# One-hot windows of 32 nodes, one group each, in a four-layer graph network kernel

## The chip, the cores and the metric

The kernel runs on one core of one Trainium2 chip. The metric is the device time of one execution in microseconds (us), the median over several runs.

## The reference

Four layers on 625 nodes with 512 features and 20000 edges, whose target nodes `dst` are sorted. Each layer is applied to `relu(layernorm(x))` and added to `x`.

```
dst = (625 * jax.random.uniform(jax.random.fold_in(_gk, 3), (20000,)) ** 2.0).astype(jnp.int32)
_o = jnp.argsort(dst, stable=True); src = src[_o]; dst = dst[_o]
...
# layer 0: mean over incoming edges
agg = segment_sum(x[src], dst) / max(deg, 1);  out = relu(agg @ W_l.T + b_l + x @ W_r.T)
# layer 1: four transformer blocks with attention over the edges (4 heads, conditioned layer norm)
# layer 2: graph convolution, norm = dis[row] * dis[col] * sigmoid(edge_attr_3 @ conf_w.T + conf_b)
# layer 3: a network on every edge
h        = mish(concat([x[src], x[dst], edge_attr_64]) @ W1 + b1)
messages = mish(h @ W2 + b2)
agg      = segment_sum(messages, dst)
u        = mish(concat([x, agg]) @ W3 + b3);  out = layernorm(x + u @ W4 + b4) * gamma + beta
```

## The kernel before

The edges are cut, in their sorted order, into 40 **groups** of 512 (`GROUPS`), a group into four tiles of 128 edges. Since `dst` is sorted, a group has its targets in a short run of nodes. The kernel relies on that twice: a **window** of `WIN` nodes from the group's first target is compared with the targets of its edges, which gives a one-hot matrix only `WIN` columns wide, and a product with this matrix sums the edges onto the window.

- `front` builds the three dense 640 x 640 adjacency matrices (`sums`: counts, and weights in a high and a low part). VectorE (DVE) makes the source one-hots (`compare_from`, L607, three tiles of a group; ScalarE makes the fourth with `Abs` and `Relu`, L371 and L374) and the target one-hots (`compare_to`, L599). GpSimd (POOL) multiplies these by the edge weights (L350). TensorE (PE) multiplies source by target one-hots (L491, 20 matmuls a group) into PSUM, and DVE adds the result onto the window of `sums` (`add_span`, L627). Two groups (`SHARE = 2`) share a window of 64 nodes and one addition. The window's start is loaded from memory into a register of DVE's sequencer (`start_of`, L593, a TENSOR_LOAD with three small instructions).
- `transformer_and_gcn` is dense and isn't touched.
- `edge_layer` runs layer 3. POOL gathers the rows of both ends of each edge (L1756, L1787) by indirect DMA; PE turns them (L1861), adds the edge features (L1869, L1870) and multiplies by W2 (L223); ScalarE (ACT) and DVE compute two `mish` functions per pair of tiles (`step`, one step for each of 80 pairs, two steps a group); PE sums a group's messages onto its window (L1901, in two column halves of the array, `side`); DVE copies the sums out of PSUM (L2131), and POOL adds them onto the table in memory (L1801). The last four groups are summed in another way (L1885).

The width of the window is made safe by **sweeps**. The kernel takes the largest difference between a span's last and first target, counts in how many of the thresholds `WIN`, `2 WIN`, ... are at or below it, and loads that count `n` on each engine. All loops then run over `n + 1` times the 40 groups: sweep `w` repeats the whole work with each window moved on by `w * WIN` nodes.

```
step(dve.tensor_scalar(over[:, :], iota16[0:1, WIN:NP:WIN], span1[:, 0:1], None, ALU.is_le))
step(dve.tensor_reduce(span1[:, 1:2], over[:, :], AX.X, ALU.add))
with dve.Fori(0, n * (GROUPS // RING) + (GROUPS // RING - 1)) as t:           # front
with eng.Fori(0, n * (PAIRS // 4) + (PAIRS - DEPTH) // 4 - 1) as t:           # edge_layer, PAIRS = 80
```

Of the kernel before, what the change touches and what calls it, by code (L numbers as in the profile page):

```python
# [21 lines left out]
P = 128  # L22
# [13 lines left out]
SHARE = 2  # L36
# [3 lines left out]
WIN = 64  # L40
# [191 lines left out]
def front(nc, k):  # L232

    RING = 4
    PEELED = 5
    ctx = ExitStack()
    with ctx:
# [6 lines left out]
        shared = sb("shared", [1, 2, SPANS])  # L244
        wtab = sb("wtab", [1, (MAXSWEEPS + 1) * GROUPS])
# [8 lines left out]
        to_onehot = [sb(f"to_onehot{a}", [P, TPG, 3, WIN], F16) for a in range(RING)]  # L254
# [4 lines left out]
        own_part = sb("own_part", [P, NT, D])  # L259
        eps, neg_mean, var = k.eps, sb("neg_mean", [P, NT]), sb("var", [P, NT])  # L260
# [51 lines left out]
        with nc.Block() as block:  # L312
# [23 lines left out]
            def _(pool):  # L336
# [6 lines left out]
                with pool.Fori(0, n * (GROUPS // RING) + GROUPS // RING) as t:  # L343
                    for a in range(RING):
# [4 lines left out]
                        weights = wb[:, bass.ds((t * RING + a) % GROUPS * TPG, TPG), :]  # L349
# [119 lines left out]
            def _(pe):  # L469
# [10 lines left out]
                with pe.Fori(0, n * (GROUPS // RING) + GROUPS // RING) as t:  # L480
                    for a in range(RING):
# [4 lines left out]
                        first, last = a % SHARE == 0, a % SHARE == SHARE - 1  # L486
                        if first:
                            pe.wait_ge(added, t * (RING // SHARE) + (a // SHARE + 1))
                        for i in range(NT):
                            for j in range(TPG):  # L490
                                mm = pe.matmul(ps[a // SHARE % 2][:, i * 4 * WIN:i * 4 * WIN + 3 * WIN],  # L491
                                               from_onehot[a][:, j, i * P:(i + 1) * P],
                                               to_onehot[a][:, j, :, :].rearrange("p a b -> p (a b)"),
                                               start=(first and j == 0 and i % 2 == 0), stop=(last and j == TPG - 1 and (i % 2 == 1 or i == NT - 1)))
# [42 lines left out]
            def _(dve):  # L537
# [30 lines left out]
                own(dve.tensor_reduce(shared[:, 0, :], cols(ps_row[:, 0, :], SHARE), AX.X, ALU.min))  # L568
                step(dve.tensor_reduce(shared[:, 1, :], cols(ps_row[:, 1, :], SHARE), AX.X, ALU.max))
# [1765 lines left out]
```

## Time and profile before

| | us |
|---|---|
| median of 3 runs | 1642.54 (1638.32 to 1642.61) |
| the profiled execution | 1639.68 |
| its span, first to last instruction | 1638.0 |

| stretch of the span, us | what runs |
|---|---|
| 0 to 104 | windows, weights and the loop of `front` |
| 104 to 862 | the rest of `front`, transformer and graph convolution |
| 862 to 975 | tables and the first steps of `edge_layer` |
| 975 to 1545 | the steady part of the edge steps |
| 1545 to 1638 | last steps and the end |

The views name an engine's own work by its name (PE, DVE, ACT, POOL) and its sequencer's by a q behind it (DVEq). The time of an instruction runs from its start to its end, and successive ones on an engine may overlap by some tens of nanoseconds.

### The profile page before, as it was taken

How to read it: one execution, taken by the hardware profiler on the slowest of the kernel's cores; microseconds unless marked ns; L12 is line 12 of the kernel's file. 1: busy time of each engine (PE TensorE's matmuls, PEld its weight loads, DVE VectorE, ACT ScalarE, POOL GpSimd, SP SyncE). 2: the span in 40 equal slices, each digit the busy share in tenths (PEclk: the TensorE clock that was granted, in tenths of full speed). 3: DMA queues.
4: the chain of work that ended last, by engine and by line, in shares of the span. 5: the costliest groups of instructions: out<-in, count | busy, mean ns of one | idle time of the engine just before them, and what ended most of it. 6: DMA issues, size and time to landing. Idle time of an engine off the chain costs nothing. (4 is left out here: it accounts for less than half of the span.)

```text
span 1638.0 us, 25185 instructions
## 1 busy us (share of the span) xinstructions
PE 1549.4 (95%) x8530; PEld 1226.5 (75%) x8530; DVE 1193.1 (73%) x1976; ACT 1097.3 (67%) x1534; POOL 672.7 (41%) x498
## 2 busy tenths in 40 slices
PE   5789899999999999999999999999999999999987
PEld 4765586878788878877854778787878787888774
DVE  8977646555565646465623499999999999999967
ACT  9841546544554546444530599999999999999963
POOL 3410200120012001200302788888888888888601
PEclk9999899999999999999999999999999999999989
DMA  3001320022012201212106767777777777777710
GB/s 106 0 20 66 92 83 26 15 68 87 26 33 84 77 1 33 81 36 78 41 1 222 160 142 148 146 150 150 148 152 148 152 150 148 149 149 150 170 39 32
DMA packets 107048, 153.95 MB, mean 94 GB/s; under 512 B 42043, under 2 KB 47035, under 8 KB 106467
## 3 DMA queue, kind: packets, MB, share of 16 engines
q0 software_dynamic: 72832, 87.84, 28.4%
q1 hardware_dynamic: 34146, 65.21, 12.6%
q8 instruction: 41, 0.67, 0.2%
q14 instruction: 29, 0.23, 0.0%
HBM read 141.02 MB, written 11.73 MB: 93 GB/s over the span
## 5 line engine op out<-in xcount | busy, mean ns | idle before, releaser
L1787 POOL DMA_INDIRECT edge_gathered<-dst_table,edge_index x158 | 262.0, 1658 | 58.7 <-issue 54.4
L223 PE MATMUL edge_z2p<-edge_w_hi,edge_h_hi 128*128 128x512 f32 x628 | 253.3, 403 | 2.6 <-DVE edge_late L2117 2.6
L223 PE MATMUL edge_z2p<-edge_w_lo,edge_h_hi 128*128 128x512 f32 x628 | 249.0, 396 | 0.0
L223 PE MATMUL edge_z2p<-edge_w_hi,edge_h_lo 128*128 128x512 f32 x628 | 248.8, 396 | 0.0
L1756 POOL DMA_INDIRECT edge_gathered<-src_table,edge_index x158 | 201.8, 1277 | 85.4 <-POOL edge_index L1750 30.6
L977 POOL TENSOR_TENSOR h<-h,tr_row_b 128x512 f32<-128x512 f32 x40 | 59.3, 1520 | 271.4 <-ACT C L1222 271.1
L966 POOL TENSOR_TENSOR tr_cw<-w_c,tr_cw 32x1024 fp32r<-32x1024 f32 x7 | 16.6, 2375 | 348.7 <-ACT tr_cw L1182 348.7
L223 PEld LDWEIGHTS edge_z2p<-edge_w_hi,edge_h_hi 128*128 128x128 f32 x628 | 118.4, 189 | 42.0 <-issue 16.9
L223 PEld LDWEIGHTS edge_z2p<-edge_w_hi,edge_h_lo 128*128 128x128 f32 x628 | 118.5, 189 | 28.5
L223 PEld LDWEIGHTS edge_z2p<-edge_w_lo,edge_h_hi 128*128 128x128 f32 x628 | 118.5, 189 | 25.0
L2134 DVE SCALAR_TENSOR_TENSOR edge_early<-edge_early,edge_z1p 128x1024 f32<-128x1024 f32 x79 | 96.4, 1220 | 48.9 <-ACT edge_early L2002 48.8
L993 PE MATMUL tr_one<-tr_yT_hi,tr_w_hi 128*128 128x256 f32 (+2 forms) x384 | 119.5, 311 | 4.4 <-issue 4.3
L993 PE MATMUL tr_one<-tr_yT_lo,tr_w_hi 128*128 128x256 f32 (+2 forms) x384 | 118.7, 309 | 0.0
L993 PE MATMUL tr_one<-tr_yT_hi,tr_w_lo 128*128 128x256 f32 (+2 forms) x384 | 118.7, 309 | 0.0
L1277 ACT ACTIVATE hT<-hT,tr_nmax 128x626 f32<-128x626 f32 x56 | 45.7, 817 | 95.3 <-DVE tr_nmax L1461 94.6
L2117 DVE TENSOR_TENSOR edge_late<-edge_z2p,w_c 128x512 f32<-128x512 f32 x157 | 101.7, 682 | 9.3 <-PE edge_z2p L223 5.0
L1998 ACT ACTIVATE edge_early<-edge_early 128x1024 f32<-128x1024 f32 x79 | 83.8, 1061 | 27.1 <-DVE edge_early L2090 26.9
L2145 DVE TENSOR_TENSOR edge_h_lo<-edge_early,edge_h_hi 128x1024 fp32r<-128x1024 f32 x79 | 96.8, 1225 | 2.7
L1075 PE MATMUL tr_two<-tr_kT,tr_qT 128*128 128x313 f32 x320 | 98.3, 433 | 0.2
L2097 DVE SCALAR_TENSOR_TENSOR edge_late<-edge_late 128x1024 f32<-128x1024 f32 x79 | 95.7, 1212 | 0.3 <-ACT edge_late L2011 0.3
L1461 DVE CUSTOM_DVE_ANT_0 hT<-tr_two,logc 128x626 f32<-128x626 f32 x80 | 64.6, 807 | 36.2 <-PE tr_two L1075 36.0
L2014 ACT ACTIVATE edge_late<-edge_late 128x1024 f32<-128x1024 f32 x79 | 84.0, 1063 | 4.6 <-DVE edge_late L2137 1.9
(366 smaller groups left out, 4020.0 us busy)
## 6 DMA issues: line engine op xcount, KB each, us to landing
w_c<-in_attr_T SPq DMA_DIRECT2D x78, 128.0 KB, 4.1
agg<-edge_sum_rows POOLq DMA_DIRECT2D x36, 128.0 KB, 10.7
w_a<-in_wv SPq DMA_DIRECT2D x4, 1024.0 KB, 5.3
w_b<-in_wq SPq DMA_DIRECT2D x4, 1024.0 KB, 5.4
w_a<-in_wk SPq DMA_DIRECT2D x4, 1024.0 KB, 7.7
w_b<-in_wo SPq DMA_DIRECT2D x4, 1024.0 KB, 6.8
w_a<-in_m SPq DMA_DIRECT2D x4, 1024.0 KB, 5.4
w_b<-in_m SPq DMA_DIRECT2D x4, 1024.0 KB, 5.5
```

What stands on the lines that cost most here:

```text
L223: mm = pe.matmul(out, a, b, start=(n == 0), stop=(n == last))
L993: mm = pe.matmul(out, a, b, start=(start and n == 0), stop=(stop and n == len(terms) - 1))
L1075: mm = pe.matmul(bank[:, f, 0:PART_A], qT[:, h, i * P:(i + 1) * P], kT[:, h, f * PART_A:(f + 1) * PART_A], start=True, stop=True)
L1461: ins = dve.tensor_tensor_reduce(out=cols(scores[n % 2][:, 0:USED], PART_A), in0=bank[:, :, 0:PART_A], in1=cols(k.logc[:, i, 0:USED], PART ...
L1756: pool.indirect_dma_start(out=from_rows[a][:, j, :].bitcast(F32), out_offset=None, in_=k.src_table, in_offset=bass.IndirectOffsetOnAxis(ap ...
L1787: pool.indirect_dma_start(out=from_rows[ring][:, j, :].bitcast(F32), out_offset=None, in_=k.dst_table, in_offset=bass.IndirectOffsetOnAxis ...
L1998: act.activation(m1[one], m1[one], ACT.Square).then_inc(S["inner1_ready"], 1)
L2014: act.activation(m2[two], m2[two], ACT.Square).then_inc(S["square2_ready"], 1)
L2097: dve.scalar_tensor_tensor(h2[new], m2[new], 0.5, z2[new], ALU.subtract, ALU.mult).then_inc(S["h2_ready"], 1)
L2117: dve.tensor_tensor(z2[two][:, j * D:(j + 1) * D], ps_z2[:, j * D:(j + 1) * D], b2, ALU.add).then_inc(S["z2_ready"], 1)
L2134: dve.scalar_tensor_tensor(m1[one], m1[one], 0.5, ps_z1[one][:, :], ALU.subtract, ALU.mult).then_inc(S["h1_ready"], 1)
L2145: dve.tensor_tensor(h1_lo[one][:, :, :], cols(m1[one], EDGE), h1_hi[one][:, :, :].bitcast(F32), ALU.subtract).then_inc(S["lo_ready"], 1)
```

## The change

`SHARE` goes from 2 to 1 and `WIN` from 64 to 32: each group has a window of its own, 32 nodes wide. With that:

- The largest difference is now taken over single groups and compared with 32, 64, ... (19 thresholds in place of 9); the table of starts has 840 entries in place of 440, is made by one instruction in place of ten, and is made again at the head of `edge_layer`.
- `front`'s loops run in turns of eight groups (`TO_RING = 8` buffers of target one-hots); `compare_to` is made six groups ahead (`TO_AHEAD`), the addition is one for each group, half as wide, and POOL's product for a group also waits until `compare_from` of the group two before it is done.
- `edge_layer` sums a group on PE in four column quarters of 32 in place of two halves of 64, with 128 output columns each in place of 256; the copy (L2131) and the addition in memory (L1801) have half the size.

```diff
-SHARE = 2
+SHARE = 1
-WIN = 64
+WIN = 32
+SIDES = P // WIN
+PLANES = D // (4 * WIN)
...
+    TO_RING = 8
+    TO_AHEAD = 6
...
-                        pool.wait_ge(to_ready, t * RING + (a + 1))
+                        pool.wait_ge(to_ready, t * TO_RING + (a + 1))
+                        pool.wait_ge(from_ready, t * TO_RING + (a + 1))
...
-                        pe.wait_ge(from_ready, u + 1)
+                        pe.wait_ge(from_ready, u + 3)
...
-                        if first:
-                            pe.wait_ge(added, t * (RING // SHARE) + (a // SHARE + 1))
+                        pe.wait_ge(added, u + 1)
...
+                own(dve.tensor_reduce(k.first_dst[:, :], cols(ps_row[:, 0, :], SHARE), AX.X, ALU.min))
+                step(dve.tensor_reduce(shared[:, :], cols(ps_row[:, 1, :], SHARE), AX.X, ALU.max))
+                step(dve.tensor_tensor(shared[:, :], shared[:, :], k.first_dst[:, :], ALU.subtract))
...
                 step(dve.tensor_scalar(over[:, :], iota16[0:1, WIN:NP:WIN], span1[:, 0:1], None, ALU.is_le))
...
-                with dve.Fori(0, n * (GROUPS // RING) + (GROUPS // RING - 1)) as t:
-                    for a in range(0, RING, SHARE):
-                        u = t * RING + a
-                        start, start_next = start_of(u), start_of(u + RING)
-
-                        dve.wait_ge(group_ready, u + (SHARE + RING))
-                        for b in range(SHARE):
-                            compare_to(u + (RING + b), a + b, start_next)
-                        add_span(t * (RING // SHARE) + a // SHARE, a, start)
-                        for b in range(SHARE):
-                            compare_from(u + (RING + b), a + b)
+                def group_step(u, a):
+                    start, start_ahead = start_of(u), start_of(u + TO_AHEAD)
+                    dve.wait_ge(group_ready, u + (1 + RING))
+                    compare_to(u + TO_AHEAD, (a + TO_AHEAD) % TO_RING, start_ahead)
+                    add_span(u, a, start)
+                    compare_from(u + RING, a % RING)
+
+                with dve.Fori(0, n * (GROUPS // TO_RING) + (GROUPS // TO_RING - 1)) as t:
+                    for a in range(TO_RING):
+                        group_step(t * TO_RING + a, a)
...
-                        pool.dma_start(k.agg[bass.ds(start, WIN), :].rearrange("n (s c) -> s n c", s=2),
+                        pool.dma_start(k.agg[bass.ds(start, WIN), :].rearrange("n (s c) -> s n c", s=SIDES),
...
-                                for side in range(2):
-                                    mm = pe.matmul(ps_sum[slot][side * WIN:(side + 1) * WIN, 0:D // 2],
+                                for side in range(SIDES):
+                                    mm = pe.matmul(ps_sum[slot][side * WIN:(side + 1) * WIN, 0:D // SIDES],
```

In DVE's program, inside `front`'s loop, half a turn (two groups) read before as follows; ISA stands for the sequencer's small instructions, `w_c` and `front_from_onehot` are the source one-hots of the two groups.

```order
L593 TENSOR_LOAD starts
L593 ISA x3
L593 TENSOR_LOAD starts
L593 ISA x2
L635 REGISTER_ALU
L599 ISA [waits front_group_ready]
L599 TENSOR_TENSOR front_to_onehot0<-front_iota16,front_dst16 128x4x64
L599 ISA
L599 TENSOR_TENSOR front_to_onehot1<-front_iota16,front_dst16 128x4x64
L625 ISA
L627 ISA [waits front_added]
L627 TENSOR_TENSOR front_sums<-front_sums,front_sum_ps0 128x15x64
```

In the same place one group reads now as follows, and every further group has the same rows again.

```order
L598 TENSOR_LOAD front_starts
L598 ISA x3
L598 TENSOR_LOAD front_starts
L598 ISA x2
L638 REGISTER_ALU
L604 ISA [waits front_group_ready]
L604 TENSOR_TENSOR front_to_onehot6<-front_iota16,front_dst16 128x4x32
L631 REGISTER_ALU
L633 ISA [waits front_added]
L633 TENSOR_TENSOR front_sums<-front_sums,front_sum_ps0 128x15x32
L612 ISA
L612 TENSOR_SCALAR w_c<-front_iota16,front_src_f 128x640
```

So the two loads of starts, which served two groups, now stand before each group; the comparison and the addition are half as large, and the addition comes once a group.

In PE's program, in a step of `edge_layer` that ends a group, the sums stood like this before, between the edge features and the product with W2:

```order
L1869 MATMUL edge_z1p<-edge_attr_parts,edge_attr_w_both 128x256
L1870 MATMUL edge_z1p<-edge_attr_parts,edge_attr_w_rest 128x256
L1901 MATMUL edge_sump<-edge_late,edge_onehot 64x256 x8
L223 MATMUL edge_z2p<-edge_w_hi,edge_h_hi 128x512
L223 MATMUL edge_z2p<-edge_w_lo,edge_h_hi 128x512
```

and stand like this now:

```order
L1879 MATMUL edge_z1p<-edge_attr_parts,edge_attr_w_both 128x256
L1880 MATMUL edge_z1p<-edge_attr_parts,edge_attr_w_rest 128x256
L1911 MATMUL edge_sump<-edge_late,edge_onehot 32x128 x16
L225 MATMUL edge_z2p<-edge_w_hi,edge_h_hi 128x512
L225 MATMUL edge_z2p<-edge_w_lo,edge_h_hi 128x512
```

Their place is the same; there are twice as many, each with a quarter of the output.

## Rows read from the trace of the kernel before

**Rows 1.** Busy time of each engine in five stretches of the span.

```profile
core 0: us, PE busy (x) PEld busy (x) DVE busy (x) ACT busy (x) POOL busy (x), PEclk, DMA share, GB/s
20.00:104.00 84.00, 67.37 (x780) 63.14 (x777) 81.51 (x169) 65.02 (x101) 36.68 (x36) 1.00 0.00 0
104.00:862.00 758.00, 722.12 (x3623) 570.86 (x3623) 440.02 (x877) 362.98 (x742) 84.15 (x53) 0.99 0.16 51
975.00:1545.00 570.00, 568.01 (x3279) 456.95 (x3274) 523.99 (x684) 543.78 (x548) 467.32 (x339) 1.00 0.77 152
```

**Rows 2.** Additions in front's loop, all of them (duration; first and last start).

```profile
L627 DVE TENSOR_TENSOR front_sums<-front_sums,front_sum_ps x20: 1137/1141/1155, 22.5 to 102.9; 128x960 f32 x20
```

**Rows 3.** Front's loop, instructions in time order: start, duration.

```profile
60.86 0.75 DVE L599 TENSOR_TENSOR front_to_onehot<-front_iota,front_dst 128x256 f16 x2
61.53 1.14 DVE L627 TENSOR_TENSOR front_sums<-front_sums,front_sum_ps 128x960 f32 x1
61.58 2.04 POOL L350 TENSOR_TENSOR front_to_onehot<-front_to_onehot,front_wb 128x512 f16<-128x512 f16 x2 [2.30 <-DVE front_to_onehot L599]
62.60 2.68 DVE L607 TENSOR_SCALAR front_from_onehot<-front_iota,front_src_f 128x640 f16<-128x640 f16 x6
...
65.20 0.74 DVE L599 TENSOR_TENSOR front_to_onehot<-front_iota,front_dst 128x256 f16 x2
```

**Rows 4.** Source and target one-hots of the whole loop: duration min/median/max.

```profile
L607 DVE TENSOR_SCALAR front_from_onehot<-front_iota,front_src_f x90: 371/374/1200, 13.7 to 99.6; 128x640 f16<-128x640 f16 x90
```

**Rows 5.** DVE's sequencer on L593, from 65.1 to 66.7: durations, first and last start.

```profile
L593 DVEq FUSED_REGOPS  x4: 53/124/190, 65.1 to 66.3; - x4
L593 DVEq TENSOR_LOAD <-starts x2: 311/311/311, 65.2 to 65.9; - x2
L593 DVEq SEQ_ASSERT  x2: 23/23/23, 65.8 to 66.5; - x2
```

**Rows 6.** DVE's sequencer, later in that half turn: L599, then L607.

```profile
L599 DVEq FUSED_REGOPS  x2: 131/133/135, 68.0 to 68.2; - x2
...
L607 DVEq FUSED_REGOPS  x6: 53/57/64, 68.7 to 69.3; - x6
```

**Rows 7.** Front's loop on PE and ACT, in time order.

```profile
61.85 1.81 PE L491 MATMUL front_sum_ps<-front_to_onehot,front_from_onehot 128*128 128x192 f16 x20
...
62.30 0.83 ACT L371 ACTIVATE front_away<-front_iota,front_src_neg 128x640 f16<-128x640 f16 x1 [0.75 <-PE front_sum_ps L491]
...
63.92 0.83 ACT L371 ACTIVATE front_away<-front_iota,front_src_neg 128x640 f16<-128x640 f16 x1
```

**Rows 8.** The chain that ended last, 1190 to 1220 us, by line.

```profile
by line: PE edge_z2p L223 73.6%; PE edge_sump L1901 10.0%; PE edge_z1p L1861 6.4%; PE edge_z1p L1869 5.5%; PE edge_z1p L1870 4.7%
```

**Rows 9.** Edge steps, 1041 to 1493 us: the second mish instruction of DVE, one a step.

```profile
L2134 DVE SCALAR_TENSOR_TENSOR edge_early<-edge_early,edge_z1p x55: 1220/1221/1224, 1040.6 to 1491.6; 128x1024 f32<-128x1024 f32 x55
```

**Rows 10.** Who waited for whom, 1041 to 1493 us: total, times, longest.

```profile
DVE edge_early L2134 <- ACT edge_early L2002: 29.7, 54, 0.8
...
ACT edge_early L1998 <- DVE edge_early L2090: 15.4, 27, 0.6
```

**Rows 11.** Two edge steps on DVE and ACT, in time order.

```profile
1191.02 1.22 DVE L2134 SCALAR_TENSOR_TENSOR edge_early<-edge_early,edge_z1p 128x1024 f32<-128x1024 f32 x1 [0.77 <-ACT edge_early L2002]
...
1199.09 1.22 DVE L2134 SCALAR_TENSOR_TENSOR edge_early<-edge_early,edge_z1p 128x1024 f32<-128x1024 f32 x1 [0.32 <-ACT edge_early L2002]
...
1203.53 0.87 DVE L2090 TENSOR_SCALAR edge_early<-edge_early 128x1024 f32<-128x1024 f32 x1
...
1204.43 1.06 ACT L1998 ACTIVATE edge_early<-edge_early 128x1024 f32<-128x1024 f32 x1 [0.57 <-DVE edge_early L2090]
...
1206.62 1.06 ACT L2002 ACTIVATE edge_early<-edge_early 128x1024 f32<-128x1024 f32 x1
```

**Rows 12.** A group's sums on PE, and the matmuls around them.

```profile
1205.49 0.28 PE L1870 MATMUL edge_z1p<-edge_attr_parts,edge_attr_w_rest 128*128 128x256 f32 x1
1205.75 1.95 PE L1901 MATMUL edge_sump<-edge_late,edge_onehot 128*64 128x256 f32 x16
1207.63 0.50 PE L223 MATMUL edge_z2p<-edge_w_hi,edge_h_hi 128*128 128x512 f32 x1
```

More of the change, by code:

```diff
@@ L611, in _ @@
                 dve.wait_ge(inputs_ready, 3)
-                for a in range(SHARE):
+                dve.sem_inc(from_ready, 2)
+                for a in range(2):
                     compare_from(a, a)
                 n = sweeps(dve)
-                for a in range(0, RING, SHARE):
-                    start = start_of(a)
-                    for b in range(SHARE):
-                        compare_to(a + b, a + b, start)
-                for a in range(SHARE, RING):
+                for a in range(2):
+                    compare_to(a, a, start_of(a))
@@ L620, in _, with add_span @@
+                for a in range(2, RING):
                     compare_from(a, a)
+                for a in range(2, TO_AHEAD):
+                    compare_to(a, a, start_of(a))
                 dve.wait_ge(sums_zero, NT)
-                def add_span(s, a, start):
-                    dve.wait_ge(added, s + 2)
+                def add_span(u, a, start):
+                    dve.wait_ge(added, u + 2)
                     into = sums[:, :, :, bass.ds(start, WIN)]
-                    dve.tensor_tensor(into, into, ps[a // SHARE % 2][:, 0:NT * 4 * WIN].rearrange(
+                    dve.tensor_tensor(into, into, ps[a % 2][:, 0:NT * 4 * WIN].rearrange(
@@ new lines, in _ @@
+                with dve.Fori(0, n * (GROUPS // TO_RING) + (GROUPS // TO_RING - 1)) as t:
+                    for a in range(TO_RING):
+                        group_step(t * TO_RING + a, a)
+                for a in range(TO_RING - RING):
+                    group_step(n * GROUPS + (GROUPS - TO_RING + a), a)
+                for a in range(TO_RING - RING, TO_RING):
+                    u = n * GROUPS + (GROUPS - TO_RING + a)
+                    start = start_of(u)
+                    dve.wait_ge(group_ready, u + (1 + RING))
+                    add_span(u, a, start)
@@ L1586, in edge_layer @@
         onehot = [sb(f"onehot{a}", [P, TPG, WIN]) for a in range(2)]
-        sum_rows = [sb(f"sum_rows{a}", [P, D // 2]) for a in range(2)]
+        sum_rows = [sb(f"sum_rows{a}", [P, D // SIDES]) for a in range(2)]
         own_part = sb("own_part", [P, KF, NP])
@@ L1766, in _ @@
                     gather_src(a)
+                pool.wait_ge(S["last_ready"], 1)
                 pool.wait_ge(dst_stored, 16 * NT)
@@ L2068, in _ @@
                 own(dve.tensor_copy(iota[:, :], iota_i[:, :]))
+                own(dve.memset(wtab[:, :], 0.0))
+                own.wait()
+                spans = [1, MAXSWEEPS, GROUPS]
+                own(dve.tensor_tensor(wtab[:, 0:MAXSWEEPS * GROUPS].rearrange("p (w g) -> p w g", g=GROUPS),
+                                      iota[0:1, 0:NP:WIN][:, :, None].to_broadcast(spans),
+                                      k.first_dst[:, None, :].to_broadcast(spans), ALU.add))
+                own.wait()
+                dve.tensor_scalar(starts[:, :], wtab[:, :], float(NP), None, ALU.min).then_inc(S["last_ready"], 1)
                 dve.wait_ge(S["made"], 2)
```

67 lines of the change are left out of this document (30 added, 37 removed).

## The prediction

> **What bounds the kernel now.** I read the busy times by stage first. In `front`'s loop DVE is busy 81.51 of 84 us, in the steady edge steps PE 568, ACT 544 and DVE 524 of 570 us; the 758 us between them are not touched by the change [rows 1]. So two places count.
>
> In `front`'s loop DVE's instructions follow each other without a gap: one turn of two groups runs from the comparison at 60.86 to the next at 65.20, 4.34 us or 2.17 a group [rows 3]. PE waits between groups and ACT has slack, two of its `Abs` lying 1.62 us apart [rows 7]. In the edge steps the chain that ended last runs over PE alone [rows 8]. But a busy PE is not the whole story: 54 of 55 times DVE's L2134 waited for ACT's L2002, 29.7 us in all, and ACT's L1998 waited for DVE's L2090 every second time, 15.4 us in all [rows 10]. Followed in time, L2134 at 1191.02 and at 1199.09 both wait for ACT, the next one comes after L1998, L2000 and L2002 end at 1207.68, and L1998 itself had waited for L2090 [rows 11]. That is a ring of DVE and ACT in which PE has no part, and it takes 8.1 and 8.6 us, together the period that the steps have: 451.0 us over 54 steps, 8.35 a step, 16.70 a group [rows 9]. PE and the ring are about equally long.
>
> **The change, part by part.** *The number of sweeps.* This decides everything else, so it comes first. A group needs a second sweep when its last target minus its first is 32 or more, since a window of 32 nodes holds a difference of 31. I drew `dst` as the reference does and cut it into groups of 512. The density of targets thins out towards the end (the square of a uniform number), and the differences grow from 0 in the first group to 28 to 32 in the last full ones. The largest is in the 39th group: nodes 590 to 622, a difference of 32. The threshold test is "32 at or below 32", which is true, so `n` becomes 1. Before, with pairs of groups, the largest difference is 59, below 64, and `n` is 0; the trace agrees, with 20 additions for 40 groups [rows 2] and one L2134 for each of 79 pairs. With `n` = 1 every loop that runs over groups, in `front` and in `edge_layer`, runs 80 groups in place of 40, whatever the window of a group holds: nothing is skipped. One node too many in one group of 40 costs a full second pass.
>
> *`front`'s loop, per group.* On DVE's own queue: the comparison of two groups takes 60.86 to 61.53, 0.67 us, so a half-sized one some 0.20; the addition lies 1.07 us ahead of what follows, half of it some 0.56; three clean source one-hots are 3 x 0.30 = 0.89, taking the starts within the six [rows 3]. Of the 90 and 30 such instructions the median is 374 ns, and one reached 1200 [rows 4]: it stood behind the addition while POOL's second product ran, 61.58 to 63.62 [rows 3]. The change puts POOL's product beside the addition, so I take all three clean. Sum 1.65 us a group. The Trainium skill (SBUF — State Buffer, "Who interferes with whom") says that DVE and GpSimd share a port pair as an exclusive lock and the loser blocks fully; by that rule this part should be a gain, of 0.4 us a group, and I have counted it so.
>
> But DVE's sequencer works too. It made the two loads of starts between 65.1 and 66.6, 1.5 us (TENSOR_LOADs at 65.2 and 65.9, the last assertion at 66.5) [rows 5]. The comparison's instruction takes 0.2 (68.0 to 68.2), from there to the source one-hots 0.5 for the second comparison and the addition, and these 0.13 each (68.7 to 69.3 for six) [rows 6]. Before, one pair of loads served two groups: 1.5 + 0.7 + 0.8 = 3.0 of 4.34 us, hidden under DVE's queue. Now every group has its own pair: 1.5 + 0.2 + 0.2 + 0.4 = 2.3 us, less a little where the groups' small instructions drop out, 2.25. That is longer than DVE's 1.65 and than ACT's 1.62, so I expect the sequencer to become the bound of this loop, at 2.25 a group; PE's 20 matmuls took 1.81 [rows 7] and can only get shorter with 96 columns in place of 192. The halved work saves nothing here. The first addition can start some 2 us earlier, at 20.5, as it needs one group and not two. 76 groups at 2.25 and the last four at PE's pace, 1.3 each, give 20.5 + 171 + 5 = 196.5. Before, the last addition ended at 104.0 [rows 2]. So **+93 us**. Bounds: 1.65 a group if the sequencer is somehow covered, +47; 2.4 if its extra waits cost time, +104.
>
> *Edge steps, per group.* The group's 16 matmul records take 1205.75 to 1207.63, 1.88 us [rows 12]. They come in two halves of the array side by side. With four quarters and half the columns the streaming halves: some 0.9 us less if four run side by side as two do, nothing less if they don't. DVE's copy of the sums halves too, by some 0.13. Since the ring of ACT and DVE stays as it is, PE's gain goes mostly into a wait of PE; I take 16.6 us a group in place of 16.70. The most that could come is a period of ACT's own busy time: 543.78 us in 570 [rows 1], which is 15.9 a group. The least is 16.8 (POOL's or PE's added instructions disturbing). The Trainium skill (TensorEngine Tiling (Array Packing), "Theoretical Speedup") promises up to 4x for at most 32 output columns of the stationary side; were PE the sole bound, that would give 0.9 us times 76 groups, 68 us, and more than ACT allows. The ring says otherwise, and that is a rival below.
>
> With a second sweep, 40 more groups run at the steady pace: 40 x 16.6 = 664 us; the 36 old ones in this form save 36 x 0.1 = 4. So **+660 us**.
>
> *The rest.* The table of starts (one instruction in place of ten, but 840 entries converted) comes out even to within 1 us; its second making at the head of `edge_layer` runs on DVE while PE's table products are long. The late groups' matmuls become smaller in columns, but not in weights. All of it I put at 0, with 2 us either way.
>
> **Sum.** 1639.7 (the profiled execution) + 93 + 660 = 2393 us. The profiled execution lies 3 us under the median, inside the spread of the three runs; I leave that out.
>
> **Rivals.**
>
> 1. *No second sweep* (the other side: not slower). All of the above hangs on one difference of 32. If the inputs on the chip have at most 31 in every group, `n` stays 0. For it: an older setting of the random generator draws other targets from the same seed, and with it I count a largest difference of exactly 31; nothing in this trace tells the two draws apart, as pairs of groups stay below 64 in both. A window chosen at 32 would fit such inputs. Against it: the generator as it stands gives 32. Then `front`'s loop ends at 20.5 + 36 x 2.25 + 5 = 106.5, +2.5 us, and the edge steps save 4: 1638, no change; if the ring gives way to ACT's 15.9 a group, 36 x 0.8 = 29 less, 1613. It decides between 31 and 32, with nothing between. 0.10, half of it on each of the two times.
>
> 2. *PE was the true bound in the edge steps*, as the chain of waits says [rows 8], and ACT's and DVE's waits for each other are slack that closes up once PE is faster. Then the period falls to ACT's 15.9: 40 x 15.9 - 36 x 0.8 = 607, in all 2340 us. Against it: PE isn't named among the waits of L2134 or L1998 [rows 10]. 0.12.
>
> 3. *`front`'s loop follows DVE's queue and not its sequencer*, 1.65 us a group: 2347 us. Against it: the loads' times are measured, and their number is in the program. 0.08.
>
> The forecast, 2393, has 0.68, with a range of its own from 2375 to 2415; 0.02 is left for what I don't see.
>
> **How the numbers follow.** Rivals 2 and 3 reach down to 2340; their halves or both together with a part of each lie above 2325. The upper bounds of both prices give 1639.7 + 104 + 676 = 2420. The range 2325 to 2420 holds the forecast and rivals 2 and 3, 0.88 less what is left for misjudged sizes. A difference of 0.3% (5 us) is about what can be told from none here. Slower by more is all with two sweeps and the rest: 0.89. Rival 1 splits into 0.05 within 0.3% and 0.06 faster.
>
> **What would show it.** Two sweeps: 80 additions in `front` in place of 20, 80 products on POOL, 159 in place of 79 of each instruction per step in `edge_layer`, and about 36 + 40 = 76 additions in memory. The front's loop: starts of DVE's additions 2.25 us apart with idle time on DVE ahead of the comparison, `front`'s last addition near 196 us. Clean source one-hots, all near 374 ns. The edge steps: L2134's counterpart still waiting for ACT, 16.6 us a group; PE busy for some 15.6 of them, with a wait ahead of the sums. The prediction is wrong from its root if the additions count 40; in its front part if they stand 1.7 us apart; in its edge part if the period is below 16.3.

## The result and the profile after

The kernel after takes 2390.03 us (median of four runs, 2389.54 to 2390.43), the kernel before on the same chip 1640.64 us: a ratio of 1.4577, with a 95% interval from 1.4558 to 1.4597. Predicted were 2393 us. The profiled execution has a span of 2388.6 us.

The two instructions that count the groups come first: the additions in `front` (L633, was L627) and the second `mish` instruction of a step in `edge_layer` (L2154, was L2134); duration min/median/max in ns, then the first and the last start.

```profile
L633 DVE TENSOR_TENSOR front_sums<-front_sums,front_sum_ps x80: 640/643/656, 21.6 to 195.8; 128x480 f32 x80
L2154 DVE SCALAR_TENSOR_TENSOR edge_early<-edge_early,edge_z1p x159: 1220/1221/1223, 1010.9 to 2318.6; 128x1024 f32<-128x1024 f32 x159
```

The same view of the kernel before, for the step instruction alone (its additions are in [rows 2]):

```profile
L2134 DVE SCALAR_TENSOR_TENSOR edge_early<-edge_early,edge_z1p x79: 1208/1221/1224, 917.2 to 1567.9; 128x1024 f32<-128x1024 f32 x79
```

80 additions and 159 steps: two sweeps. These rows also divide the 750.6 us between the two spans. `front`'s last addition ends at 196.4 in place of 104.0, +92.4. From there to the first L2154 it is 814.5 in place of 813.2, +1.3. The steps take 1307.7 in place of 650.7, +657.0. What follows the last one has 70.0 in place of 70.1.

Busy time by stretch, the counterpart of [rows 1]: both halves of `front`'s loop together, the untouched middle, the steady edge steps.

```profile
core 0: us, PE busy (x) PEld busy (x) DVE busy (x) ACT busy (x) POOL busy (x), PEclk, DMA share, GB/s
20.00:196.00 176.00, 124.05 (x1560) 111.08 (x1560) 149.79 (x384) 126.91 (x180) 47.49 (x77) 0.61 0.00 0
196.00:955.00 759.00, 722.52 (x3622) 570.31 (x3622) 440.56 (x876) 362.83 (x741) 84.09 (x52) 0.99 0.16 51
1068.00:2300.00 1232.00, 1193.59 (x8318) 980.44 (x8317) 1116.93 (x1488) 1180.33 (x1190) 1009.77 (x740) 1.00 0.73 148
```

In the middle nothing moved. In `front`'s loop DVE is no longer full (149.79 of 176 us), and one number was not in the prediction: the granted clock of PE is 0.61 there, where it was 1.00. In the edge steps PE is busy for 1193.59 of 1232 us.

`front`'s loop in time order, to be read beside [rows 3]:

```profile
60.32 0.61 POOL L356 TENSOR_TENSOR front_to_onehot<-front_to_onehot,front_wb 128x256 f16<-128x256 f16 x1 [1.89 <-DVE w_c L612]
60.37 0.70 DVE L604 TENSOR_TENSOR front_to_onehot<-front_iota,front_dst 128x128 f16 x1 [0.34 <-issue]
61.00 0.64 DVE L633 TENSOR_TENSOR front_sums<-front_sums,front_sum_ps 128x480 f32 x1
...
61.56 0.97 DVE L612 TENSOR_SCALAR front_from_onehot<-front_iota,front_src_f 128x640 f16<-128x640 f16 x3
61.79 1.76 PE L495 MATMUL front_sum_ps<-front_to_onehot,front_from_onehot 128*128 128x96 f16 x20 [0.74 <-DVE front_sums L633]
...
62.71 0.29 DVE L604 TENSOR_TENSOR front_to_onehot<-front_iota,front_dst 128x128 f16 x1 [0.18 <-issue]
62.82 0.65 POOL L356 TENSOR_TENSOR front_to_onehot<-front_to_onehot,front_wb 128x256 f16<-128x256 f16 x1 [1.89 <-DVE front_from_onehot L612]
62.92 0.65 DVE L633 TENSOR_TENSOR front_sums<-front_sums,front_sum_ps 128x480 f32 x1
```

DVE idles ahead of each comparison with the releaser "issue": it waits for nothing that the profile shows. What it waits for is its own sequencer, which is still at the loads of the starts. These are the loads ahead of the comparison at 60.37, and the sequencer's instruction for that comparison (durations, first and last start):

```profile
L598 DVEq TENSOR_LOAD <-front_starts x2: 300/302/303, 58.8 to 59.6; - x2
L604 DVEq FUSED_REGOPS  x1: 135/135/135, 60.2 to 60.2; - x1
```

Where POOL's product starts first (60.32), the comparison behind it takes 0.70 us and ends 0.14 us after it; where the comparison is first (62.71), it takes 0.29. The addition beside the product stays at 0.65. So additions stand 2.50 or 1.9 us apart, 2.205 in the mean ((195.8 - 21.6) / 79). The last few, behind the loop, come faster: the 76th starts at 191.0, which makes 2.26 us a group up to there, and a whole turn of eight groups takes 18.2 us, 2.28 a group.

The edge steps in the waits of the stretch from 1200 to 2200 us (total, times, longest), beside [rows 10], and PE's sums of a group, beside [rows 12]:

```profile
DVE edge_early L2154 <- issue: 78.7, 121, 0.8
...
ACT edge_early L2008 <- issue: 30.5, 53, 0.6
PE edge_sump L1911 <- DVE edge_late L2117: 26.0, 60, 0.5
```

```profile
1712.07 1.08 PE L1911 MATMUL edge_sump<-edge_late,edge_onehot 128*32 128x128 f32 x32 [0.45 <-DVE edge_late L2117]
1713.08 0.50 PE L225 MATMUL edge_z2p<-edge_w_hi,edge_h_hi 128*128 128x512 f32 x1
```

The sums now hold PE for 1.01 us in place of 1.88, and PE waits 0.45 us ahead of them, once a group. DVE still waits before every L2154, ACT before every second L2008 (the counterpart of L1998): 53 times in this row and 7 in one that names L2110. The rows call most of these waits "issue"; on the two engines the instruction before them in the ring ends just ahead of each, L2012 of ACT and L2110 of DVE:

```profile
1704.29 1.06 ACT L2012 ACTIVATE edge_early<-edge_early 128x1024 f32<-128x1024 f32 x1
...
1710.75 1.06 ACT L2008 ACTIVATE edge_early<-edge_early 128x1024 f32<-128x1024 f32 x1 [0.58 <-issue]
```

```profile
1705.39 1.22 DVE L2154 SCALAR_TENSOR_TENSOR edge_early<-edge_early,edge_z1p 128x1024 f32<-128x1024 f32 x1 [0.54 <-issue]
...
1709.30 0.69 DVE L2173 TENSOR_TENSOR edge_attr_parts<-w_c,edge_attr_parts 64x512 fp32r<-64x512 f32 x1
1710.02 0.70 DVE L2110 TENSOR_SCALAR edge_early<-edge_early 128x1024 f32<-128x1024 f32 x1
...
1714.02 1.22 DVE L2154 SCALAR_TENSOR_TENSOR edge_early<-edge_early,edge_z1p 128x1024 f32<-128x1024 f32 x1 [0.76 <-issue]
```

In refit (below), which runs the same edge steps in one sweep, the view of 1000 to 1500 us names the same two waits by these instructions (L2014 and L2112 there), 61 of 61 times and 30 times:

```profile
DVE edge_early L2156 <- ACT edge_early L2014: 39.8, 61, 0.9
...
ACT edge_early L2010 <- DVE edge_early L2112: 17.2, 30, 0.6
```

### The profile page after: what moved, and what is told of

Its sections match the earlier page's. It is cut to its first block, busy times and chain, and to the rows that moved or that the text cites. A ratio compares the mean times of both kernels' runs of the same rounds, so it can differ in the third digit from the quotient of the medians.

```text
span 2388.6 us, 43137 instructions
## 1 busy us (share of the span) xinstructions
PE 2226.2 (93%) x14386; PEld 1793.3 (75%) x14386; DVE 1851.7 (78%) x2992; ACT 1793.1 (75%) x2254; POOL 1219.0 (51%) x938
## 4 chain that ended last, share of the span: by engine, by line
DVE 27%; issue 23%; PE 4%; DVEq 3%; ACT 2%; DMA 0%; POOL 0%; POOLq 0%
DVE edge_h_hi L2163 5%; DVE edge_late L2137 5%; DVE edge_early L2154 4%; DVE edge_late L2117 4%; DVE edge_early L2110 3%; DVE edge_attr_parts L2173 2%; PE edge_z2p L225 2%; DVEq L2120 2%; PE edge_z1p L225 1%; DVE edge_attr_parts L2104 1%; DVE edge_late L2157 1%; DVE edge_h_lo L2165 1%; DVE edge_sum_rows L2151 1%; DVE edge_onehot L2127 1%; PE edge_sump L1895 0%
## 5 line engine op out<-in xcount | busy, mean ns | idle before, releaser
L1797 POOL DMA_INDIRECT edge_gathered<-dst_table,edge_index x318 | 511.5, 1608 | 107.5 <-issue 96.3
L225 PE MATMUL edge_z2p<-edge_w_hi,edge_h_hi 128*128 128x512 f32 x1268 | 517.6, 408 | 9.8 <-DVE edge_late L2137 3.9
L225 PE MATMUL edge_z2p<-edge_w_hi,edge_h_lo 128*128 128x512 f32 x1268 | 501.6, 396 | 0.0
L225 PE MATMUL edge_z2p<-edge_w_lo,edge_h_hi 128*128 128x512 f32 x1268 | 501.2, 395 | 0.0
L1765 POOL DMA_INDIRECT edge_gathered<-src_table,edge_index x318 | 383.4, 1206 | 154.1 <-issue 66.2
L225 PEld LDWEIGHTS edge_z2p<-edge_w_hi,edge_h_lo 128*128 128x128 f32 x1268 | 238.3, 188 | 57.4
L2154 DVE SCALAR_TENSOR_TENSOR edge_early<-edge_early,edge_z1p 128x1024 f32<-128x1024 f32 x159 | 194.2, 1221 | 112.2 <-issue 98.5
L225 PEld LDWEIGHTS edge_z2p<-edge_w_lo,edge_h_hi 128*128 128x128 f32 x1268 | 238.6, 188 | 50.3
L2008 ACT ACTIVATE edge_early<-edge_early 128x1024 f32<-128x1024 f32 x159 | 168.1, 1057 | 50.6 <-issue 38.5
L974 POOL TENSOR_TENSOR tr_cw<-w_c,tr_cw 32x1024 fp32r<-32x1024 f32 x7 | 16.6, 2378 | 350.1 <-ACT tr_cw L1190 350.1
L2012 ACT ACTIVATE edge_early<-edge_early 128x1024 f32<-128x1024 f32 x159 | 168.6, 1060 | 5.1
L2010 ACT ACTIVATE edge_early<-edge_early 128x1024 f32<-128x1024 f32 x159 | 168.3, 1058 | 5.0
L1879 PE MATMUL edge_z1p<-edge_attr_parts,edge_attr_w_both 128*128 128x256 f32 x636 | 169.5, 299 | 1.1 <-DVE edge_attr_parts L2173 1.1
L2024 ACT ACTIVATE edge_late<-edge_late 128x1024 f32<-128x1024 f32 x159 | 169.2, 1064 | 0.9 <-issue 0.9
L2018 ACT ACTIVATE edge_late<-edge_late 128x1024 f32<-128x1024 f32 x159 | 166.0, 1044 | 3.4 <-DVE edge_late L2137 3.4
L2005 ACT ACTIVATE edge_late<-edge_late 128x1024 f32<-128x1024 f32 x159 | 167.1, 1051 | 0.1
L2021 ACT ACTIVATE edge_late<-edge_late 128x1024 f32<-128x1024 f32 x159 | 166.2, 1046 | 0.0
```

What stands on the lines that cost most here:

```text
L225: mm = pe.matmul(out, a, b, start=(n == 0), stop=(n == last))
L1765: pool.indirect_dma_start(out=from_rows[a][:, j, :].bitcast(F32), out_offset=None, in_=k.src_table, in_offset=bass.IndirectOffsetOnAxis(ap ...
L1797: pool.indirect_dma_start(out=from_rows[ring][:, j, :].bitcast(F32), out_offset=None, in_=k.dst_table, in_offset=bass.IndirectOffsetOnAxis ...
L1879: pe.matmul(z1[:, c, :], attr_w_both[:, chunk], attr_parts[slot][:, pair], start=False, stop=False)
L2008: act.activation(m1[one], m1[one], ACT.Square).then_inc(S["inner1_ready"], 1)
L2010: act.activation(m1[one], m1[one], ACT.Ln, bias=1.0).then_inc(S["inner1_ready"], 1)
```

## The experiments

The theory: the second sweep, set off by one difference of 32, is nearly the whole cost; in `front`'s loop DVE's sequencer sets the pace; in the edge steps it is the ring of DVE and ACT. The rivals: the small windows cost by themselves; `front`'s loop is bound by PE, or by POOL's product in the way of the comparison; the edge steps are bound by PE. Ratios are to the kernel before, measured on the same chip in the same rounds (1638.1 to 1638.4 us), with their 95% interval.

### The number of sweeps

**plus_sweep.** The kernel before, made to sweep twice.

```
-                dve.tensor_copy(k.sweeps[:, :], span1[:, 1:2]).then_inc(windows_known, 1)
+                dve.tensor_scalar(k.sweeps[:, :], span1[:, 1:2], 1.0, None, ALU.add).then_inc(windows_known, 1)
```

> The kernel before with one sweep more (groups in pairs, windows of 64, all else as before). If the second sweep alone is what the change costs, the loop of front grows by 40 groups of 2.17 us, 87 us, and the edge steps by 40 groups of 16.70 us, 668 us: about 2395 us, within 0.5% of the kernel after. If the smaller windows or the second pair of loads had a large share of the 750 us, this kernel would stand well below 2390.

Measured: 2394.79 us, 1.4615 (1.4592 to 1.4638). The wide windows with two sweeps are as slow as the narrow ones, to 0.2%.

**minus_sweep.** The kernel after, made to sweep once.

```
-                step(dve.tensor_scalar(over[:, :], iota16[0:1, WIN:NP:WIN], span1[:, 0:1], None, ALU.is_le))
+                step(dve.tensor_scalar(over[:, :], iota16[0:1, WIN:NP:WIN], span1[:, 0:1], None, ALU.is_lt))
```

> The kernel after, with the threshold test 'at or below' turned to 'below', so that a difference of exactly 32 starts no second sweep; left out is the sum of the edges whose target is node 622 in the 39th group. If the sweep is the whole cost: front's last addition ends at 21.6 + 39 x 2.205 + 0.64 = 108.2 in place of 104.0 (+4.2), the middle +1.3 as measured, the edge steps -4 by a period of 16.58 in place of 16.70: 1641 to 1643 us, no difference to before. Rival (the edge steps bound by PE, period 15.9): 1613 us. Rival (half-sized windows cost by themselves): over 1650 us.

Measured: 1634.43 us, 0.9974 (0.9959 to 0.9989). Some 7 us better than expected: the last addition starts at 104.7 and not at 107.6 (the last four groups have one load each in place of two, and no comparison or source one-hots in their way; they follow each other by 0.85 to 1.45 us, and the expectation had counted every group at the mean of eighty), and the 78 steps take 644.5 us in place of 650.7.

**refit.** One sweep by the data: 32 empty places moved into the 39th group.

```
-LAST_EDGES = EDGES - (GROUPS - 1) * GROUP
+LAST_EDGES = 64
+FILL_AT = EDGES - LAST_EDGES
+FILL = (GROUPS - 1) * GROUP - FILL_AT
...
-        a = np.concatenate([a, np.full((pad,) + a.shape[1:], fill, a.dtype)])
+        a = np.concatenate([a[:FILL_AT], np.full((FILL,) + a.shape[1:], fill, a.dtype), a[FILL_AT:],
+                            np.full((pad,) + a.shape[1:], fill, a.dtype)])
...
```

> The kernel after, with 32 of the empty places moved from the end of the last group to the end of the 39th, whose real edges then reach a difference of 31 only; the last group holds 64 edges. The kernel counts one sweep by itself and computes the whole result. Expected: as minus_sweep, 1641 to 1643 us, within 0.2% of it. If something other than the count of sweeps made the kernel slow, it would stay near 2390.

Measured: 1632.95 us, 0.9965 (0.9953 to 0.9978), like minus_sweep. The whole computation is done, in one sweep, because 32 edges moved to the next group. All 757 us between it and the kernel after hang on the 39th group's last node.

### `front`'s loop

**carry_start.** refit with one load of a start per group.

```
+                start_regs = [dve.alloc_register(f"start{a}") for a in range(TO_RING)]
-                def start_of(u):
-                    return dve.value_load(starts[0:1, bass.ds(u, 1)], min_val=0, max_val=NP)
+                def start_of(u, a):
+                    dve.reg_load(start_regs[a], starts[0:1, bass.ds(u, 1)])
+                    return kept_start(a)
+                def kept_start(a):
+                    return dve.snap(start_regs[a], min_val=0, max_val=NP)
...
-                    start, start_ahead = start_of(u), start_of(u + TO_AHEAD)
+                    start, start_ahead = kept_start(a), start_of(u + TO_AHEAD, (a + TO_AHEAD) % TO_RING)
...
```

> As refit, and in front's loop each start is loaded once into one of eight registers and kept for the addition six groups later: one load a group and no assertions in place of two loads. If DVE's sequencer is the bound of that loop (2.2 us a group), the loop falls to DVE's own queue, 1.65 us a group with clean comparisons and 1.9 with the comparison as POOL's product lengthens it: 12 to 22 us less than refit, 1620 to 1630 us. Rival (PE is the bound, its 20 matmuls of 1.8 us at a granted clock of 0.6 and the hand-over to the addition): 0 to 3 us less.

Measured: 1615.03 us, 0.9856 (0.984 to 0.9871), 18 us less than refit. That gain lies within the 12 to 22 us; the time lies under the 1620 to 1630 us because refit itself had come out some 8 us under its own expectation. The additions of refit and of carry_start, then carry_start's loop in time order:

```profile
L635 DVE TENSOR_TENSOR front_sums<-front_sums,front_sum_ps x40: 641/644/656, 21.4 to 104.6; 128x480 f32 x40
```

```profile
L641 DVE TENSOR_TENSOR front_sums<-front_sums,front_sum_ps x40: 640/642/656, 18.7 to 87.1; 128x480 f32 x40
```

```profile
69.28 0.28 DVE L612 TENSOR_TENSOR front_to_onehot<-front_iota,front_dst 128x128 f16 x1
69.48 0.64 DVE L641 TENSOR_TENSOR front_sums<-front_sums,front_sum_ps 128x480 f32 x1
...
70.05 0.99 DVE L620 TENSOR_SCALAR front_from_onehot<-front_iota,front_src_f 128x640 f16<-128x640 f16 x3
70.27 1.01 PE L497 MATMUL front_sum_ps<-front_to_onehot,front_from_onehot 128*128 128x96 f16 x20 [0.66 <-DVE front_sums L641]
...
70.96 0.28 DVE L612 TENSOR_TENSOR front_to_onehot<-front_iota,front_dst 128x128 f16 x1
```

DVE has no gap left here, and a group takes 1.68 us from comparison to comparison: the 1.65 that the prediction had worked out for DVE's queue and set aside as a rival. Seven groups between 41.6 and 57.8 us take longer, 1.9 to 2.8 us (see the last section). PE's 20 matmuls take 1.01 us here and took 1.76 in much of refit, so this run alone doesn't rule out PE's lower clock as the cause of refit's pace; the turns below do.

**early_product.** refit without POOL's wait for the source one-hots.

```
-                        pool.wait_ge(from_ready, t * TO_RING + (a + 1))
```

> As refit, but POOL's product for a group no longer waits for the source one-hots of the group two before, so it follows the comparison at once. If DVE's sequencer sets the pitch of front's loop (2.2 us a group), front's last addition stays within 1.5 us of refit's 104.6 us. Rival (the pitch comes from POOL's product, which starts 0.30 us behind the last source one-hot and stretches the comparison until it ends: 2.50 us from addition to addition in the trace): the last addition moves by more than 5 us, to 90 to 100 us if the comparison is clean and nothing else stretches, or past 110 if the product now stretches the additions or source one-hots.

Measured: 1633.97 us, 0.9967 (0.9954 to 0.9979). The product now runs beside the source one-hots, and two things change that nearly cancel: the comparison is clean (292 ns in the mean from 30 to 100 us, 474 in refit), the three one-hots take 1.21 us in place of 0.97. The last addition starts at 104.8 us, in refit at 104.6:

```profile
69.96 0.61 POOL L357 TENSOR_TENSOR front_to_onehot<-front_to_onehot,front_wb 128x256 f16<-128x256 f16 x1 [1.57 <-DVE front_to_onehot L605]
70.14 1.21 DVE L613 TENSOR_SCALAR front_from_onehot<-front_iota,front_src_f 128x640 f16<-128x640 f16 x3
...
71.60 0.29 DVE L605 TENSOR_TENSOR front_to_onehot<-front_iota,front_dst 128x128 f16 x1 [0.25 <-issue]
```

Since the two cancel, the last addition alone would not tell DVE's sequencer from DVE's queue. The idle time does: from 30 to 100 us DVE stands idle ahead of the comparisons for 8.8 us here and for 9.9 in refit, collision or not (4.3 and 1.6 of it are put down to PE). And the turn of the loop on the sequencer is the same in three kernels. These are the branches at its end, between 36 and 174 us in the kernel after, between 30 and 100 us in refit and then in early_product; from the first to the last of a row it is 18.2 us a turn:

```profile
L643 DVEq COMPARE_BRANCH  x8: 56/56/73, 37.7 to 165.3; - x8
```

```profile
L645 DVEq COMPARE_BRANCH  x4: 50/56/73, 37.6 to 92.3; - x4
```

```profile
L644 DVEq COMPARE_BRANCH  x4: 50/56/73, 37.8 to 92.5; - x4
```

The same turn rules PE out. In the kernel after the turn from 92.4 to 110.6 us ran wholly at the lower clock; in refit PE had the full clock from 52 to 58.6 us, its 20 matmuls taking 1.01 us and not 1.76, and the eight groups from 51.4 to 69.7 took 18.2 us all the same:

```profile
92.40:110.60 18.20, 14.03 (x160) 12.60 (x160) 15.65 (x42) 12.52 (x16) 4.97 (x8) 0.50 0.00 0
```

```profile
52.00:58.60 6.60, 3.03 (x60) 2.68 (x60) 5.57 (x16) 5.97 (x9) 1.86 (x3) 1.00 0.00 0
```

So the collision of product and comparison shapes the intervals but not their sum; the sequencer sets that.

### The edge steps

**low_part_early.** refit with DVE's low part of the edge features (L2173 in the kernel after) in the wait before the second `mish` instruction (L2154 there, L2164 here).

```
+                    if a % 2 == 0 and on(0):
...
+                        dve.wait_ge(S["attr_high"], g(-2))
+                        dve.tensor_tensor(attr_parts[slot][high, :], attr[slot][high, :], attr_parts[slot][high, :].bitcast(F32),
+                                          ALU.subtract).then_inc(S["attr_low"], 1)
                     if on(2):
                         dve.wait_ge(S["q1_ready"], s(-1))
                         dve.scalar_tensor_tensor(m1[one], m1[one], 0.5, ps_z1[one][:, :], ALU.subtract, ALU.mult).then_inc(S["h1_ready"], 1)
...
-                    if a % 2 == 0 and on(0):
...
-                        dve.wait_ge(S["attr_high"], g(-2))
-                        dve.tensor_tensor(attr_parts[slot][high, :], attr[slot][high, :], attr_parts[slot][high, :].bitcast(F32),
-                                          ALU.subtract).then_inc(S["attr_low"], 1)
```

> As refit, and in edge_layer DVE's subtraction for the low part of the edge features (0.69 us, every second step) stands ahead of the second mish instruction, where DVE waits 0.54 us for ACT in every such step, and no longer between the high and low parts of h and the next step's cap, where ACT waits 0.58 us. If the ring of DVE and ACT sets the period of the edge steps, it falls from 16.58 to 16.0 to 16.1 us a group: 38 groups, 18 to 22 us less than refit, 1611 to 1615 us. Rival (PE, or something else outside this ring, sets it): 0 to 3 us less.

Measured: 1620.95 us, 0.9888 (0.987 to 0.9906), 12 us less than refit: the ring is right, the size is not. The period went from 16.58 to 16.24 us (487.2 us over 60 steps between 1000 and 1500 us), and not to 16.05. The row it is from, then DVE over the longer half of the period:

```profile
L2164 DVE SCALAR_TENSOR_TENSOR edge_early<-edge_early,edge_z1p x61: 1220/1222/1223, 1006.5 to 1493.7; 128x1024 f32<-128x1024 f32 x61
```

```profile
1298.85 1.22 DVE L2164 SCALAR_TENSOR_TENSOR edge_early<-edge_early,edge_z1p 128x1024 f32<-128x1024 f32 x1 [0.83 <-ACT edge_early L2014]
...
1306.41 0.69 DVE L2160 TENSOR_TENSOR edge_attr_parts<-w_c,edge_attr_parts 64x512 fp32r<-64x512 f32 x1
1307.13 1.22 DVE L2164 SCALAR_TENSOR_TENSOR edge_early<-edge_early,edge_z1p 128x1024 f32<-128x1024 f32 x1
```

Between the two L2164 DVE works without a gap, 8.28 us from start to start. It was a ring with a wait on either side; with the wait filled, DVE's own work is the bound of this half. The other half, 16.24 less 8.28, is about the 7.95 us that it was before the move too.

**before_low_part_early.** The same move in the kernel before.

> The same move of the low part in the kernel before (groups in pairs, sums in two halves of 1.88 us). If PE was as long as the ring there, as its 568 busy of 570 us say, the period can only fall from 16.70 to about 16.64 us: 2 us less than before, 1636 to 1639 us, no difference that counts. Rival (the ring alone was the bound before too): 18 to 20 us less, as in low_part_early.

Measured: 1636.8 us, 0.999 (0.9981 to 0.9999), as expected. The same edit is worth 12 us with the quick sums and 1 us with the slow ones: in the kernel before PE was as long as the ring, and with the ring shortened it is busy all the time. The period fell by 0.11 us a group, to 16.59, and the last steps gave it back (651.5 us from the first `mish` row to the last, 650.7 before). The view of 1000 to 1500 us:

```profile
1000.00:1500.00 500.00, 500.00 (x2892) 402.99 (x2891) 462.12 (x603) 479.04 (x483) 411.24 (x302) 1.00 0.73 151
```

**double_sums.** low_part_early with every group's sums made twice on PE.

```
+                        for b in range(2):
+                            for j in range(PT):
+                                for side in range(SIDES):
+                                    mm = pe.matmul(ps_sum[slot][side * WIN:(side + 1) * WIN, 0:D // SIDES],
+                                                   onehot[slot][:, b * PT + j, :],
+                                                   h2[b][:, j * D + side * (D // SIDES):j * D + (side + 1) * (D // SIDES)],
+                                                   start=(b == 0 and j == 0), stop=(b == 1 and j == PT - 1))
                         for b in range(2):
```

> low_part_early with every group's sums on PE done twice into the same place (32 matmuls of 128 columns in place of 16, the second round starts anew), about 1.0 us more on PE a group and nothing more on any other engine. If PE is nearly as long as the period (16.0 of 16.24 us), the period rises to 17.0 us: 36 groups by 0.76, 27 us more than low_part_early, 1645 to 1651 us. Rival (the ring of DVE and ACT alone sets it and PE has room): less than 5 us more.

Measured: 1643.43 us, 1.0023 (1.001 to 1.0035), 22 us more than low_part_early, where 27 was expected; the period is 16.85 us, not 17.0. PE had 7.3 us of room in the stretch from 1000 to 1500 us, where it was busy 492.69 us without the second round, and now has none:

```profile
1000.00:1500.00 500.00, 499.96 (x4291) 419.46 (x4293) 445.62 (x592) 471.75 (x476) 413.34 (x298) 1.00 0.72 144
```

So PE's own work was 0.24 us a group short of the period in low_part_early. This run does not say what holds the 16.24.

**carry_and_low_part.** refit with the edits of carry_start and low_part_early.

> refit with both: one load of a start per group kept in registers (which took 18 us off refit) and the low part early in the edge steps. The two stages follow one after the other, so their gains add: 1595 to 1599 us if low_part_early brings 18, 1612 to 1616 if it brings nothing.

Measured: 1601.16 us, 0.9765 (0.9751 to 0.978), the fastest version here. The gains add, 18 and 12 us, to within 2 us (32 us less than refit); it misses the 1595 to 1599 because low_part_early brought 12 us and not 18.

**onehot_shift.** carry_and_low_part with DVE's target one-hot one step earlier.

```
-                    if a % 2 == 0 and on(6):
-                        start = dve.value_load(starts[0:1, bass.ds(g(6), 1)], min_val=0, max_val=NP)
...
+                    if a % 2 == 1 and on(5):
+                        start = dve.value_load(starts[0:1, bass.ds(g(5), 1)], min_val=0, max_val=NP)
```

> carry_and_low_part, and DVE's target one-hot of a group (0.28 us, with its load of a start) is made one step earlier, where DVE waits 0.83 us for ACT, and no longer ahead of the low part. In low_part_early the low part starts only 0.24 us too late, since the two additions, the copy of the sums and the low part end behind ACT's exponentials, and the period stays at 16.24 us. If that lateness is what is left, the period falls to PE's own 16.0 us (492.7 busy of 500 us at 16.24), 37 groups by 0.17 to 0.24: 6 to 9 us less than carry_and_low_part, 1592 to 1595 us. Rival (PE or ACT is the bound at 16.24 already): 1600 to 1602 us.

Measured: 1603.92 us, 0.9783 (0.9768 to 0.9798), on another chip, where the kernel before is 0.3 us slower; 3 us more than carry_and_low_part and not 6 to 9 less. The one-hot's old place had cost nothing: the period is 16.32 us and not lower. DVE from the h2 product to the two additions, in low_part_early and then in onehot_shift:

```profile
1303.52 1.25 DVE L2119 SCALAR_TENSOR_TENSOR edge_late<-edge_late 128x1024 f32<-128x1024 f32 x1
1304.69 0.28 DVE L2129 TENSOR_TENSOR edge_onehot<-edge_iota,dst_f 128x128 f32 x1
1304.89 1.29 DVE L2139 TENSOR_TENSOR edge_late<-edge_z2p,w_c 128x512 f32<-128x512 f32 x2
```

```profile
1301.71 1.23 DVE L2125 SCALAR_TENSOR_TENSOR edge_late<-edge_late 128x1024 f32<-128x1024 f32 x1
1303.09 1.29 DVE L2133 TENSOR_TENSOR edge_late<-edge_z2p,w_c 128x512 f32<-128x512 f32 x2
```

1.37 us from one to the other with the one-hot between them, 1.38 without: the additions wait for the end of the h2 product, and the one-hot had filled that wait. Of the 3.2 us between the two spans 1.1 lie in the edge steps (633.2 us from the first second `mish` instruction to the last, 632.1 before the move) and the rest mostly in `front` and the middle, whose code is the same. Why the period rose from 16.25 stays open.

## Why the prediction was right, point by point

- **Two sweeps.** Right, and the whole of the cost: the step was read from the reference's targets and the test `is_le`, not from the trace. plus_sweep and refit show it from both sides.
- **`front`'s loop, 2.25 us a group by DVE's sequencer, +93.** Right: 2.26 us for the 76 groups and +92.4. That the last addition ends at 196.4 where 196.5 was worked out is partly luck: the first one starts at 21.6 and not at 20.5, the 76 groups take 1.5 us less than worked out, the last four 0.4 more. carry_start and the turns show the cause. Two details of the step were wrong without weight in the sum. All of DVE's instructions were taken as clean: the source one-hots are (median 375 ns), but the comparison now stands in POOL's way (278/518/748 ns over the loop), since the late sequencer brings it just behind the product's start. And PE's matmuls could "only get shorter", which they hardly did: they took 1.76 us at a granted clock of 0.50 (58 to 66 us), against 1.81 before with twice the columns.
- **Edge steps, 16.6 us a group, +660.** Right: 994.7 us over 120 steps from L2154's rows between 1200 and 2200, 16.58 a group, +657.0. The ring of DVE and ACT held the period while PE's sums got 0.87 us shorter. One sign was off: PE was to be busy for some 15.6 us a group and was for 16.1 (968.98 of 1000 us from 1200 on); its busy time, 16.6 before, fell by less than its sums did, and why stays open.
- **Its rival, PE as the true bound, 15.9.** Out: the period stayed, and PE waits 0.45 us ahead of the sums. It held a part of the truth: before_low_part_early shows that PE was the second bound at the same height.
- **The rest at 0.** 1.3 us in the middle, -0.1 at the end.
- **Rival 1, without the second sweep 1638 or 1613.** 1633: what was priced was the ring's case, with +2.5 us in `front` (refit has +1.2) and -4 in the steps (-6.0).

This is the view that gives the 16.58 (first and last start in the stretch):

```profile
L2154 DVE SCALAR_TENSOR_TENSOR edge_early<-edge_early,edge_z1p x121: 1220/1221/1223, 1200.1 to 2194.8; 128x1024 f32<-128x1024 f32 x121
```

## What to carry to other kernels

Where a kernel repeats all of its work when the data pass a bound, work out the bound on the data before costing anything else; here one node in one group cost 757 us, and moving 32 edges across a border undid it. When instructions are halved and doubled in number, add up the sequencer's share of each (its loads of registers, its assertions, its loop turn) beside the engine's queue. And where two bounds have the same height, shortening one alone shows nothing: change both, or measure each with the other already moved. When two effects of an experiment may cancel, as in early_product, an unmoved time proves little; look for a quantity that one of the rivals alone can hold fixed, here the turn of the sequencer's loop.

## What the runs showed of the hardware

- A load of a start into DVE's register takes 0.30 to 0.32 us, and a pair of them with its register operations and assertions 1.5 us; leaving out one of the two and the assertions took the steady part of `front`'s loop from 2.28 to 1.68 us a group, where DVE's own queue became the bound.
- PE's granted clock fell to the lower level (0.50, which is 1.2 GHz) in `front`'s loop, in the kernel after for most of it. Ahead of its first group there PE had waited 2.78 us:

```profile
22.35 1.54 PE L495 MATMUL front_sum_ps<-front_to_onehot,front_from_onehot 128*128 128x96 f16 x20 [2.78 <-ACT front_from_onehot L380]
```

  In the kernel after and in refit this cost nothing in the steady turns, as the two turns of early_product's section show. In the traces of the kernel after, minus_sweep, refit, carry_start, early_product and low_part_early the 20 matmuls of a group took 1.01 us where a record gives the full clock and 1.76 where it gives the lower one. The clock records of refit begin at 34.8 us, so the 1.00 that a view gives for a stretch before is no reading; two groups there took 3.53 us, as at the lower clock. Why the clock fell stays open.
- In carry_start the clock was at 0.50 from 43.4 to 57.0 us, and seven groups from 41.6 to 57.8 took 1.9 to 2.8 us in place of 1.68, 4.4 us in all. That is not shown to be the clock's doing. The first of them, 2.63 us long, began at the full clock, with PE waiting for ACT's one-hot; and from 42.5 to 52.0 ACT put one piece of the layer norm (L410) between its one-hots, five times, 0.81 + 0.74 + 0.80 us with no gap and 2.19 us a group. PE at the first of them:

```profile
42.65 1.14 PE L497 MATMUL front_sum_ps<-front_to_onehot,front_from_onehot 128*128 128x96 f16 x20 [2.22 <-ACT front_from_onehot L382]
```

- A comparison of DVE in half precision from two tiles in SBUF that starts behind POOL's product ends with it (0.28 us alone, up to 0.75); an addition out of PSUM beside the same product keeps its 0.64. That goes with what the Trainium skill says (SBUF — State Buffer, "SBUF: two separate sides"): the pair of ports is locked by whichever starts first, a DVE instruction with two inputs in SBUF among them, and the other blocks. A source one-hot that starts behind the product is held too: in early_product the first of each three takes up to 0.616 us in place of 0.375 and ends 0.18 us after the product, the other two are clean. The same wait is in [rows 4], with 1200 ns behind a product of 1040. The row is that of 30 to 90 us:

```profile
L613 DVE TENSOR_SCALAR front_from_onehot<-front_iota,front_src_f x58: 373/375/616, 29.8 to 89.2; 128x640 f16<-128x640 f16 x58
```

- Sums in four column quarters of the array took 1.01 us where two halves took 1.88: a factor of 1.9, where the sums of one group go from two column parts of the array to four.
